# Keys and queries of an attention kernel from four matmuls a chunk, with a GpSimd copy of both

## The reference

```python
q = einsum('oc,bcn->bon', Wq, xf) + bq[None, :, None]     # 32 channels
k = einsum('oc,bcn->bon', Wk, xf) + bk[None, :, None]     # 32 channels
v = einsum('oc,bcn->bon', Wv, xf) + bv[None, :, None]     # 256 channels
att = softmax(einsum('bdi,bdj->bij', q, k) / sqrt(32), axis=-1)
out = gamma * einsum('bcj,bij->bci', v, att)
fused = einsum('oc,bchw->bohw', Wf, concatenate([out, x], axis=1)) + bf
```

## Time and profile before

| | |
|---|---|
| Runs | 2089.87, 2091.38, 2096.21 us; median 2091.38 |
| Profiled execution | 2091.23 us, span 2089.1 us, mean granted PE clock 0.993 |
| PE | 2040.8 us busy (98%), 16208 matmuls |
| ACT | 1752.5 us busy (84%) |
| DVE | 1589.7 us busy (76%) |
| POOL | 1204.9 us busy (58%), 868.0 us idle waiting for `top_m` |
| Chain that ended last | PE 79%, issue 8%, DVE 7%, ACT 4% |

### The profile page before, as it was taken

The page is one execution under the profiler, slowest core; times in us unless marked ns, Lnnn a source line. Parts: engine busy times, 40 slices in busy tenths (PEclk is TensorE's granted clock), DMA queues, the critical chain, the costliest instruction groups (busy, mean ns, idle before and its releaser), DMA issues.

```text
span 2089.1 us, 44966 instructions
## 1 busy us (share of the span) xinstructions
PE 2040.8 (98%) x16208; PEld 1992.9 (95%) x16208; DVE 1589.7 (76%) x2157; ACT 1752.5 (84%) x2373; POOL 1204.9 (58%) x514
## 2 busy tenths in 40 slices
PE   8899999999989999999999999999999999999999
PEld 7899999999889999999988999999998899999999
DVE  5788887886678788878666878887767778888885
ACT  6788888887788888888777888888877888888886
POOL 0376666677036766666703677666660466677665
PEclk9999999999999999999999999999999999999999
DMA  3200000000320000000031000000003100000000
GB/s 128 86 21 12 20 20 20 20 21 11 108 76 21 21 10 20 20 20 21 11 117 67 21 21 15 15 20 20 21 11 122 41 21 21 20 20 10 20 21 16
DMA packets 54081, 69.46 MB, mean 33 GB/s; under 512 B 4048, under 2 KB 37584, under 8 KB 53968
## 3 DMA queue, kind: packets, MB, share of 16 engines
q1 hardware_dynamic: 53696, 67.91, 10.0%
q10 hardware_dynamic: 272, 0.07, 0.0%
HBM read 34.41 MB, written 33.55 MB: 33 GB/s over the span
## 4 chain that ended last, share of the span: by engine, by line
PE 79%; issue 8%; DVE 7%; ACT 4%; DVEq 1%; DMA 0%; ACTq 0%; SPq 0%
PE ps_o L376 61%; PE ps_s L368 8%; PE ps_p L234 4%; DVE top L595 3%; PE ps_o L234 2%; ACT ps_p L529 2%; DVE o_norm L626 1%; PE ps_t L276 1%; ACT queries L466 1%; PE ps_t L234 1%; ACT hi L441 1%; PE ps_s L251 1%; PE ps_t L261 1%; PE ps_t L268 1%; DVE inv L622 1%
## 5 line engine op out<-in xcount | busy, mean ns | idle before, releaser
L736 POOL TENSOR_TENSOR raw<-raw,top_m 128x1024 f32<-128x1024 f32 x508 | 1204.2, 2410 | 868.0 <-ACT top_m L452 868.0
L614 DVE TENSOR_TENSOR lo<-ps_p,hi 128x1024 fp32r<-128x1024 f32 x512 | 626.9, 1224 | 329.7 <-ACT ps_p L529 319.3
L595 DVE TENSOR_TENSOR top<-ps_s,top 128x512 f32<-128x512 f32 x960 | 660.9, 688 | 69.6 <-ACT raw L447 14.5
L525 ACT ACTIVATE hi<-raw 128x1024 fp32r<-128x1024 f32 x512 | 543.9, 1062 | 176.7 <-PE ps_o L376 170.6
L376 PE MATMUL ps_o<-val_hi,hi 128*128 128x258 f32 x4096 | 673.7, 287 | 17.8 <-ACT hi L525 10.4
L376 PE MATMUL ps_o<-val_lo,hi 128*128 128x256 f32 x4096 | 654.5, 282 | 0.0
L376 PE MATMUL ps_o<-val_hi,lo 128*128 128x258 f32 x4096 | 602.0, 284 | 0.0
L447 ACT ACTIVATE raw<-ps_s 128x512 f32<-128x512 f32 x1024 | 554.2, 594 | 55.5 <-PE ps_s L368 32.5
L376 PEld LDWEIGHTS ps_o<-val_hi,hi 128*128 128x128 f32 x4096 | 564.6, 190 | 31.2 <-DVE o_norm L626 19.0
L376 PEld LDWEIGHTS ps_o<-val_lo,hi 128*128 128x128 f32 x4096 | 562.7, 190 | 0.0
L376 PEld LDWEIGHTS ps_o<-val_hi,lo 128*128 128x128 f32 x4096 | 541.4, 191 | 0.0
(11 more groups left out here) (63 smaller groups left out, 1029.9 us busy)
## 6 DMA issues: line engine op xcount, KB each, us to landing
xf<-x SPq DMA_DIRECT2D x32, 512.0 KB, 3.9
conv_d<-conv_st SPq DMA_DIRECT2D x64, 256.0 KB, 2.0
result<-conv_d SPq DMA_DIRECT2D x64, 256.0 KB, 2.6
out<-result SPq DMA_DIRECT2D x64, 256.0 KB, 2.2
raw<-wf2T SPq DMA_DIRECT2D x1, 256.0 KB, 4.3
raw<-wv SPq DMA_DIRECT2D x1, 256.0 KB, 4.1
raw<-wf1T SPq DMA_DIRECT2D x1, 256.0 KB, 4.9
raw<-wkqT ACTq DMA_DIRECT2D x1, 64.0 KB, 2.1
```

The lines of the kernel that those rows point to most:

```text
L525: nc.scalar.activation(hi[:, p], raw[:, slot].rearrange("p j i -> p (j i)"), ACT.Exp, scale=SCALE).then_inc(hi_done, 1)
L595: nc.vector.tensor_tensor(top[:, new], scores, top[:, new if half else old], ALU.max).then_inc(max_done, 1)
L614: nc.vector.tensor_tensor(lo[:, t % 2], ps_p[:].rearrange("p h n -> p (h n)"), hi[:, t % 2].bitcast(F32), ALU.subtract).then_inc(lo_done, 1)
L736: nc.gpsimd.tensor_tensor(raw[:, slot], raw[:, slot], top_m[:, r].unsqueeze(1).broadcast_to((P, JQ, I)), ALU.subtract).then_inc(sub_done, 1)
```

## The change

PE makes keys and queries with four matmuls a chunk instead of six: the 128 weight columns are now the 64 high columns (k, q) and beside them the 64 low ones, so `ps_p[0:64]` holds high weights times x and `ps_p[64:128]` low weights times x, both for x high and x low (this includes low x low). The two halves must be added across partitions. ACT moves the low half with the bias to a new SBUF tile `kq_low` (64 partitions). DVE adds it to the PSUM half and writes `kq` in SBUF (64 partitions; signals `kq_done`). From `kq`, ACT makes the first high group of keys and of queries, DVE the low groups (now both sources in SBUF), and POOL writes the second high group of each by two copies (signals `kq_twice`). PE waits for `kq_twice` beside `k_out` and `q_out`; DVE waits for the last `kq_twice` before it writes `kq` again. The duplicated bias `bkkqq` and its four small copies at the start go.

```diff
-        wkq_hi = sb("wkq_hi", [P, KT, 4, CK], F32R)
-        wkq_lo = sb("wkq_lo", [P, KT, 4, CK], F32R)
-        bkkqq = sb("bkkqq", [P, 1], F32)
+        wkq = sb("wkq", [P, KT, 2, 2 * CK], F32R)
+        kq = sb("kq", [2 * CK, W], F32)
+        kq_low = sb("kq_low", [2 * CK, W], F32)
...
                 def project_kq(c, C):
                     pe.wait_ge(x_split, C + 1)
-                    product3(ps_p[:, 0], lambda k: wkq_hi[:, k], lambda k: wkq_lo[:, k],
-                             lambda k: x_hi(c)[:, k, :], lambda k: x_lo(c)[:, k, :]).then_inc(kq_ready, 1)
+                    terms = [(k, x) for k in range(KT) for x in (x_hi, x_lo)]
+                    for i, (k, x) in enumerate(terms):
+                        last = nc.tensor.matmul(ps_p[:, 0], wkq[:, k].rearrange("p r u -> p (r u)"), x(c)[:, k, :],
+                                                start=(i == 0), stop=(i == len(terms) - 1))
+                    last.then_inc(kq_ready, 1)
...
                 pe.wait_ge(k_out, C + 1)
+                pe.wait_ge(kq_twice, C + 1)
                 pe.wait_ge(q_out, C + 1)
...
                 def kq_hi(c, C):
                     act.wait_ge(kq_ready, C + 1)
-                    nc.scalar.activation(keys[0:2 * CK, span(c)], ps_p[0:2 * CK, 0], ACT.Identity,
-                                         bias=bkkqq[0:2 * CK]).then_inc(k_hi_done, 1)
-                    for to in (0, 2 * CK):
-                        last = nc.scalar.activation(queries[to:to + CK, span(c)], ps_p[2 * CK:R3, 0], ACT.Identity,
-                                                    bias=bkkqq[2 * CK:R3])
-                    last.then_inc(q_hi_done, 1)
+                    nc.scalar.activation(kq_low[:], ps_p[2 * CK:P, 0], ACT.Identity, bias=bkq[2 * CK:P]).then_inc(kq_low_done, 1)
+                    act.wait_ge(kq_done, C + 1)
+                    nc.scalar.activation(keys[0:CK, span(c)], kq[0:CK], ACT.Copy).then_inc(k_hi_done, 1)
+                    nc.scalar.activation(queries[0:CK, span(c)], kq[CK:2 * CK], ACT.Copy).then_inc(q_hi_done, 1)
...
+                def add_kq(C):
+                    dve.wait_ge(kq_low_done, C + 1)
+                    if not (isinstance(C, int) and C == 0):
+                        dve.wait_ge(kq_twice, C)
+                    nc.vector.tensor_tensor(kq[:], ps_p[0:2 * CK, 0], kq_low[:], ALU.add).then_inc(kq_done, 1)
+
                 def kq_lo(c, C):
                     dve.wait_ge(k_hi_done, C + 1)
-                    nc.vector.scalar_tensor_tensor(keys[2 * CK:R3, span(c)], ps_p[0:CK, 0], bkkqq[0:CK],
-                                                   keys[0:CK, span(c)].bitcast(F32), ALU.add,
-                                                   ALU.subtract).then_inc(k_out, 1)
+                    nc.vector.tensor_tensor(keys[2 * CK:R3, span(c)], kq[0:CK], keys[0:CK, span(c)].bitcast(F32),
+                                            ALU.subtract).then_inc(k_out, 1)
                     dve.wait_ge(q_hi_done, C + 1)
-                    nc.vector.scalar_tensor_tensor(queries[CK:2 * CK, span(c)], ps_p[2 * CK:R3, 0], bkkqq[2 * CK:R3],
-                                                   queries[2 * CK:R3, span(c)].bitcast(F32), ALU.add,
-                                                   ALU.subtract).then_inc(q_out, 1)
+                    nc.vector.tensor_tensor(queries[CK:2 * CK, span(c)], kq[CK:2 * CK],
+                                            queries[0:CK, span(c)].bitcast(F32), ALU.subtract).then_inc(q_out, 1)
...
+                add_kq(C)
                 kq_lo(c, C)
...
                 if c == CHUNKS - 2:
+                    add_kq(C + 1)
                     kq_lo(c + 1, C + 1)
...
             def project(b, c, first):
+                pool.wait_ge(kq_done, snap(pool, b * CHUNKS + (c + 1)))
+                pool.sem_inc(kq_seen, 1)
+                nc.gpsimd.tensor_copy(keys[CK:2 * CK, span(c)], kq[0:CK])
+                nc.gpsimd.tensor_copy(queries[2 * CK:R3, span(c)], kq[CK:2 * CK]).then_inc(kq_twice, 1)
```

More of the change, by code:

```diff
@@ L91, in attention_conv @@
         wkq_raw = raw[:, 9, 2, 0:KT * 2 * CK].rearrange("p (k n) -> p k n", k=KT)
-        wkq_twice = raw[:, 9, 2, 0:KT * 2 * CK].rearrange("p (u c) -> p u c", c=CK).unsqueeze(2).broadcast_to(
-            (P, KT * 2, 2, CK))
         ps_s = ctx.enter_context(nc.psum_tensor("ps_s", [P, BANKS, 2, I], F32))
@@ L108, in attention_conv @@
         x_hi_done, x_split = sem("x_hi_done"), sem("x_split")
-        kq_ready, bkq_spread = sem("kq_ready"), sem("bkq_spread")
+        kq_ready, kq_low_done, kq_done, kq_twice = (sem("kq_ready"), sem("kq_low_done"), sem("kq_done"),
+                                                    sem("kq_twice"))
         k_hi_done, q_hi_done, k_out, q_out = sem("k_hi_done"), sem("q_hi_done"), sem("k_out"), sem("q_out")
+        kq_seen = sem("kq_seen")
         conv_ready, conv_done = sem("conv_ready"), sem("conv_done")
@@ L436, in _ @@
             act.wait_ge(wkq_loaded, 16)
-            nc.scalar.activation(wkq_hi[:].rearrange("p k (u r) c -> p (k u) r c", r=2), wkq_twice, ACT.Copy).then_inc(wkq_hi_done, 1)
+            nc.scalar.activation(wkq[:, :, 0], wkq_raw, ACT.Copy).then_inc(wkq_hi_done, 1)
             def split_x(b, c):
@@ L500, in project @@
                     act.wait_ge(vec_loaded, 16)
-                    act.wait_ge(bkq_spread, 1)
                 kq_hi(c, C)
@@ L558, in _ @@
             dve.wait_ge(wkq_hi_done, 1)
-            nc.vector.tensor_tensor(wkq_lo[:].rearrange("p k (u r) c -> p (k u) r c", r=2), wkq_twice,
-                                    wkq_hi[:].bitcast(F32).rearrange("p k (u r) c -> p (k u) r c", r=2), ALU.subtract).then_inc(wkq_split, 1)
-            def spread_bkq():
-                dve.wait_ge(vec_loaded, 16)
-                for g, u in enumerate((0, 0, 1, 1)):
-                    last = nc.vector.tensor_copy(bkkqq[g * CK:(g + 1) * CK], bkq[u * CK:(u + 1) * CK])
-                last.then_inc(bkq_spread, 1)
+            nc.vector.tensor_tensor(wkq[:, :, 1], wkq_raw, wkq[:, :, 0].bitcast(F32), ALU.subtract).then_inc(wkq_split, 1)
             def setup_wf2():
@@ L675, in project @@
                 if start:
-                    spread_bkq()
+                    dve.wait_ge(vec_loaded, 16)
                     split_x(0, 0)
```

## The result

| | median us (lowest to highest) | profiled span us |
|---|---|---|
| before | 2089.87 (2087.99 to 2096.21), 5 runs | 2089.1 |
| changed | 2104.23 (2103.01 to 2104.63), 5 runs | 2102.4 |

The ratio is 1.0062, 95% interval 1.0046 to 1.0078. The changed kernel is slower, by 14 us in the medians and 13.3 in the spans. The forecast was 2121, 30 us more than before: the sign is right, the size is less than half of what was forecast.

What follows compares the result with a forecast made beforehand. PE was taken to bound chunks 1 to 3 and DVE the others. With POOL and DVE hindering each other, 3 x 8.02 + 5.98 = 30.0 us on 2091.23 gave 2121 us; range 2091 to 2133.

Steps and rivals of the forecast that it cites:

- The loop through ACT and DVE: Chunks 1 to 3: from one finished kq to the next takes 7.41 us unhindered, above PE's 7.04.
- ACT's wait for `kq`: Each chunk: ACT waits about 1 us for DVE to finish kq.
- D: Each chunk: the moment DVE has finished kq, put at T + 1.43 us when unhindered.
- T: Each chunk: the moment ACT sees kq_ready, PE's signal that the key and query matmuls are done.
- The low halves and POOL: After D each chunk: POOL's two copies of 0.70 us run first, so DVE's two low-half subtractions end 0.99 us later.
- in turn: POOL's copies and DVE's low-half subtractions run one after the other: 30.0 us more, 2121 us; chance 0.60.
- free case: POOL's copies and DVE's subtractions do not hinder each other: 5.6 us more, 2097 us; chance 0.32.
- the six folds: Chunk 7: DVE's folds start at chunk 6's D + 8.49 us unhindered, D + 10.18 with hindrance.
- PE's wait ends 0.20 (1.19) later than before: Chunk 0, images 1 to 3: PE's wait for result ends 0.20 us later unhindered, 1.19 with hindrance.
- wrong if the time falls under 2105 while POOL's copies take 0.7, or if the low halves come at D + 2.1: Sign of failure: total under 2105 us with POOL copies of 0.7 us, or DVE's low halves done at D + 2.1.

Runs made afterwards that it cites:

- pool_writes: Changed kernel with POOL's two copies out of kq replaced by memsets of the same targets, so POOL writes but reads nothing: 2095.56 us, ratio 1.0013.
- six: Changed kernel with six matmuls again for keys and queries (x low term added twice), new chain kept: 2112.53 us, ratio 1.0086.
- before_four: Kernel before with four matmuls for keys and queries, the two with low weights left out, ACT and DVE work unchanged: 2078.64 us, ratio 0.9923.
- pool_late: Changed kernel with POOL's two copies held back until DVE has finished both subtractions: 2144.42 us.
- warm: Changed kernel with eight unread matmuls of 512 columns at each of two PE waits (chunk 0 of images 1 to 3, chunk 6): 2093.59 us, ratio 1.0003.
- early_result: Changed kernel with DVE's addition of the last result in chunk 0 moved ahead of the addition of kq: 2089.44 us, ratio 0.9983.
- early_both: Changed kernel with the last result added early and, in chunk 6, early scores folded between kq addition and low halves: 2086.94 us, ratio 0.9962.
- before_att: Kernel before with 16 unread matmuls of 256 columns at the start of each image's attention: 2091.14 us, ratio 0.9991.

## Why the prediction was wrong, and what in it was right

**Right: PE's saving doesn't arrive.** The loop through ACT and DVE was put at 7.41 us free, above PE's 7.04, with bounds of 7.2 to 7.5. Without hindrance, in pool_writes, it measures 7.26. In the changed kernel it is 7.50, because PE's convolution half 1 waits for the delayed `queries`; that this is exactly the old period is chance. ACT's wait for `kq` was foreseen as about 1 us and is 0.94. D was foreseen 1.43 after T and is 1.41 in chunk 0 (534.54 - 533.13). six and before_four show both halves: 0.46 us a chunk without the chain, nothing with it in chunks 1 to 3.

**The first failed step, right in kind and wrong in size: "The low halves and POOL".** The step said: in turn, "DVE's keys run from D + 1.68 to 2.37, its queries to D + 3.09, 0.99 later than free". They do take turns (pool_writes, pool_late). But the queries end at 536.92, D + 2.38, some 0.3 later than the D + 2.10 of the free case. Two things failed in this step. POOL starts at D + 0.16, not 0.25, and its first copy takes 0.60, not 0.70 (the 769 ns that the prediction quotes is further off), so it is as good as over when DVE's `keys` begins at D + 0.69. And the step let POOL do both copies in a row, although DVE's `keys` stands ready between them; it was the second copy that had to wait, and it delayed only `queries`, by 0.30. The Trainium skill, "SBUF — State Buffer", section "Who interferes with whom", says that a DVE instruction with two SBUF inputs contends with a GpSimd instruction that reads SBUF and not with one that only writes. The trace agrees: `queries` takes 0.98 beside a copy, and POOL's memset beside `keys` takes 0.52, as alone. That the later one waits for the whole of the earlier, as the prediction had it, the rows do not show: POOL's second copy ends at 536.38, 0.44 after `queries` begins, and `queries` is only 0.30 longer. What failed most is my use of the rule: it decides between instructions one by one, and I applied it to a pair.

With 0.29 in place of 0.99 the prediction's own formulas give most of what happened: the six folds at D + 8.49 + 0.29 = 8.78, and they start at 595.17, 8.78 after the D of chunk 6, 585.72 + 0.67 = 586.39; PE's wait in chunk 0 ending 0.20 + 0.29 = 0.49 later, and it ends 0.46 later against the stage's start (5.80 against 536.53 - 531.19 = 5.34). In chunks 4 and 5 the formula gives 8.71 and 8.43 is measured: the first fold starts 2.34 after low x instead of 2.46, and DVE's addition starts while the last fold still drains (577.28 against 575.08 + 2.28 = 577.36). The stage without its clock part, in warm, is 1.73 us longer than before; the free case had said 1.66. That these lie so near is in part luck, since the delay of `queries` adds and the 0.28 us less in each of chunks 4 and 5 takes away. So the chain's part is about 5 us in three images, and "in turn", which I gave 0.60, was the wrong branch by size.

**The second failed step: the clock of PE is missing.** The sum has no term for it. "PE's wait ends 0.20 (1.19) later than before" was priced as its delay alone. The wait grew from 1.83 to 2.76 us (chunk 0; 0.46 of it because PE now has two matmuls fewer and begins to wait earlier) and from 1.57 to 2.51 (chunk 7), and the matmuls behind them ran at half clock: 2.85 us an image, shown by warm, which took 10.6 us off the total. Three images give 8.6. Image 0 with its one stretch gives 1.3: from its second `kq_low` to its first exponential it takes 62.2 us in the changed kernel and 60.9 in warm. The stretch that before's profiled execution had met itself is to be taken off, about 1.5. That makes 8.4 us, with the chain's 5 about the 13.3 us of the spans. The start of the attention hardly enters: half clock there is 3.4 us longer in two of the four images, and the attention is 0.1 us shorter in one of them and 1.0 longer in the other. The Trainium skill, "TensorE: Matmul & The Clock Gate", section "HAM oscillation — how this bites in real kernels", describes a kernel whose every tile starts at the lower clock after a wait of 3 to 5 us; chunks 0 and 7 of the changed kernel show the same behind waits of 2.5 and 2.76 us, 0.50 granted behind each. Had I read the granted clock at 1111 in the kernel before (0.57), I could have made this a rival.

**The errors offset each other.** Without the overrated hindrance the forecast would have been 2097, or about 2100 by the same formulas with a delay of 0.29, under the measured time for want of the clock. The range (2091 to 2133) holds 2104 by both errors together, which is luck. The sentence "wrong if the time falls under 2105 while POOL's copies take 0.7, or if the low halves come at D + 2.1" was well aimed: the time is under 2105, with copies of 0.60 and 1.03 (mean 0.82), and the low halves are ready at D + 2.38, nearer to D + 2.1 than to D + 3.09.

**Open.** From which wait on the clock falls isn't settled, and the wait's length alone doesn't decide it. All seven waits of 2.50 to 2.76 us in the changed kernel's projection were followed by half clock, but of the four of 2.5 in early_result only two, and of the three of 2.46 in pool_writes only one. Short waits were followed by it now and then: in before's chunk 7 the wait of 1.55 in image 2, not that of 1.57 in image 1; in early_both the 1.55 of images 2 and 3; in before_att the 1.83 of chunk 0 in image 1. Before's own spread from run to run goes with its clock: of the 27 executions beside warm the eight at a mean granted clock of 0.991 took 2094.1 to 2096.9 us, the five at 0.994 took 2089.2 to 2090.4. What makes one execution meet more such stretches than another isn't known. Why the filling at the start of the attention left the clock low in image 1 wasn't tried further.

## What to carry to other kernels

Before work is taken off the busiest engine, work out the loop through the engines that answer to it; if that is longer than the bound that the saving would leave, the saving is lost, and the new chain's latency is paid at each place where the busy engine waits. Price a longer wait of PE twice, as a delay and as the half clock of the work behind it: here 0.9 us of added wait cost a further 1.3 to 1.6 us. Look for an order that shortens an old wait first: moving one DVE instruction gained 10 us by the medians, 6 of them in the stages where it was moved, while two matmuls of six gained 15 only without the chain that they need. When two engines take turns, lay their instructions out one by one with their start times; the hindrance is only where one starts while the other is at work, not the sum of all that could collide.
